# A two-layer decoder on one core: experts' outputs as rows in DRAM with gathers, three overlapping groups, a new preparation, and masks in half-array matmuls

## The chip, the cores and the metric

The kernel runs on one core of a Trainium2 chip. The metric is the time of one execution on the device in microseconds; three runs of the kernel before took 2507.99, 2510.61 and 2510.91 us (median 2510.61). Engines are named as in the profile: PE (TensorE matmul) with PEld (its weight loads), DVE (VectorE), ACT (ScalarE), POOL (GpSimd) and SP (SyncE, which here only issues DMAs).

## The reference

The input x is 64 batches of 128 tokens of 128 channels, in float32. Six blocks follow one another, each adding to x: self attention of 16 heads with a tanh cap, cross attention to 77 context tokens, and a gated feed-forward with weights quantized in groups of 16 (layer 0); a self attention with softplus weights, a cross-attention block, and a mixture of experts (layer 1). The parts that the change touches are these.

```
# layer 0, cross attention: a mask of integers, 0 or 1, per query and key
logits = q @ k.T / sqrt(dh) + (1 - mask) * -1e9      # 16 heads, 128 x 77 per batch
attn   = softmax(logits) * group_prob
# layer 0, feed-forward: each weight is quantized once, in groups of 16
sc8 = e4m3(max|w| / 6 * s);  q = sign(w) * nearest_fp4(|w| / dq) * dq
# layer 1, mixture of experts, per batch: 128 tokens, 8 experts, 2 per token, 38 slots per expert
p, e = top2(x @ router_w + router_b); p = softmax(p)
pos  = running count of e over (first choices, then second choices) - 1
inp[e, pos] += x                                     # a choice beyond slot 37 is dropped
o = (silu((inp @ w_fc + b_fc) * (inp @ w_gate + b_gate))) @ w_proj + b_proj   # 128 -> 512 -> 128
x = x + p0 * o[e0, pos0] + p1 * o[e1, pos1]          # an index beyond the last slot reads slot 37
```

## The kernel before

x stays in SBUF the whole time, as `x_resident` (tokens on partitions, 64 x 128 columns). The program is seven stages with a barrier of all engines between them: `prepare`, `l0_attention`, `l0_cross`, `l0_ffn`, `l1_attention`, `l1_cross` and `moe`. Inside a stage each engine has its own instruction stream, written out by hand, and the streams are held together by semaphores that only count up. Every engine works through its stream in order, so an instruction that waits holds all behind it.

`prepare` loads constants, weights and biases. SyncE issues the loads one by one (constants first, then the broadcast biases, the direct weights, the weights to be transposed, the three weights to be quantized, `wv` and `wp`), and after them the eight loads of x. All compute engines wait for one count over all of these loads (N_IN). PE transposes 18 weight blocks, VectorE finds the maximum of the three weights, whose reciprocal goes through PE to all partitions (L1022 to L1071), folds some weights (L1076 to L1092), and then `quantize` (L764) runs three times on VectorE, once per weight, 17 operations each that wait for one another. At the end VectorE waits for all of x.

`l0_cross` works on quads of 4 batches, with a software pipeline: `segment(c, h, p, l)` holds what each engine does for the quads at four stages. For each batch PE first writes the mask into four PSUM banks with `far` (two diagonal matrices of different size, as a single f16 can't hold the value) times `neg` (mask minus one, L1205), then adds the scores on 32-row parts of the array (L1209). VectorE takes maxima (L1476), subtracts (L1482) and sums (L1488), ScalarE takes exponentials, POOL multiplies with the gate (L1408) and the reciprocal (L1415), PE turns the weights (L1221) and multiplies with the values (L1234). VectorE makes `neg` once per quad (L1461).

`moe` works on groups of 8 batches (304 slots per expert), one pass of its loop per group. In 32 steps k (8 experts times 4 parts of the hidden 512) PE multiplies the slots of expert k//4 with w_fc and w_gate (`hidden`, L2811 and L2814), ScalarE adds the bias (L2912), VectorE adds the other bias and multiplies (L3056), ScalarE applies silu (L2919), and three steps later PE projects (`project`, L2823) with the output's channels on partitions; ScalarE moves each expert's output to `oT` (L2923). Between the steps the routing of the next group is placed: statistics and normalising on VectorE, transposes (L2777), router (L2783), top 2 (`choose`), counts (`places`) and positions (`finish`). Also between the steps VectorE builds for each batch a combine matrix of tokens by slots that holds the two probabilities (`combine`, L3042 to L3046), which PE turns (L2831) and ScalarE copies (L2928). After the steps comes a part without experts' work: for each batch PE turns the outputs to rows (L2861), ScalarE copies them (L2949), PE multiplies combine matrix and rows (L2875), VectorE adds to x (L3073), and PE makes the slots of the next group (`dispatch`, L2802) from the matrices that VectorE builds (L3032, L3034), copied by ScalarE (L2904). The next group's first step waits for all of this, as `xt`, the slots' buffer, exists once.

## Time and profile before

| | |
|---|---|
| median of three runs | 2510.61 us |
| the profiled execution | 2510.06 us |
| its span, first to last instruction | 2508.3 us |
| busy share of PE, PEld, DVE, ACT, POOL | 75%, 54%, 70%, 58%, 46% |
| mean granted clock of TensorE | 0.861 of full speed |
| DMA | 29.90 MB, mean 12 GB/s |

The stages follow one another without overlap: `prepare` to 61 us, `l0_attention` to 446, `l0_cross` to 882, `l0_ffn` to 1191, `l1_attention` to 1442, `l1_cross` to 1846, `moe` to the end. Busy shares over the whole span say little, since each stage has its own limit; a stage is read from a stretch in its middle, and from what its busiest engine waits for. A line of a timeline gives start, length, engine, line in the kernel, operation and tiles; a number behind x is how many records were merged, and brackets hold the idle time before it and what ended it. A float32 matmul has two records, one per pass. Lengths of matmuls include the way through the array, so the distance of two starts is what the engine takes for one.

### The profile page before, as it was taken

The numbers are of one execution on the slowest core, as the hardware profiler recorded it, in microseconds if no ns is written. First come the engines' busy times: TensorE is split into PE (matmuls) and PEld (weight loads), VectorE is DVE, ScalarE is ACT, GpSimd is POOL, SyncE is SP. The second block draws the span as 40 slices with busy tenths as digits, with TensorE's granted clock in tenths as the row PEclk, the third lists the DMA queues.
The fourth block names the chain that finished last, engine by engine and source line by source line (L and its number), as shares of the span: only waits on it lengthen the run. The fifth ranks groups of instructions, "written<-read, shape, count | busy, mean of one in ns | idle before, by whom it ended". The sixth has DMA issues, their size and how long they took to land. (4 is left out here: it accounts for less than half of the span.)

```text
span 2508.3 us, 50896 instructions
## 1 busy us (share of the span) xinstructions
PE 1885.9 (75%) x16165; PEld 1365.9 (54%) x16174; DVE 1762.3 (70%) x4140; ACT 1458.9 (58%) x2564; POOL 1141.6 (46%) x1090
## 2 busy tenths in 40 slices
PE   1677777699999924444556569999858988889888
PEld 1455555476767602222334347777636666666666
DVE  4799996588888679997555548888845555455553
ACT  1588887477777644554222257777725565565654
POOL 1466665488888748876111047888820000000000
PEclk7699998699999955555777779999979999999999
DMA  4000000100000030000000000000000000000000
GB/s 131 1 1 0 0 0 2 27 18 21 17 21 18 4 101 0 0 0 1 0 0 0 0 16 8 5 8 5 1 1 1 9 8 8 0 8 8 8 8 9
DMA packets 54153, 29.90 MB, mean 12 GB/s; under 512 B 18776, under 2 KB 50608, under 8 KB 54064
## 3 DMA queue, kind: packets, MB, share of 16 engines
q1 hardware_dynamic: 53920, 28.75, 4.2%
q8 instruction: 46, 0.75, 0.1%
q14 instruction: 43, 0.35, 0.0%
q10 hardware_dynamic: 144, 0.05, 0.0%
HBM read 24.60 MB, written 4.19 MB: 11 GB/s over the span
## 5 line engine op out<-in xcount | busy, mean ns | idle before, releaser
L3056 DVE SCALAR_TENSOR_TENSOR m_z<-psum,bias_col,m_hb 128x304 f32<-128x304 f32 x256 | 134.4, 532 | 208.1 <-ACT m_hb L2912 199.8
L2912 ACT ACTIVATE m_hb<-psum,bias_col 128x304 f32<-128x304 f32 x256 | 131.0, 512 | 171.6 <-PE psum L2811 171.0
L182 POOL TENSOR_SCALAR mln_ve<-mln_mv 128x4 f32<-128x4 f32 x16 | 4.5, 281 | 490.1 <-DVE mln_mv L149 490.1
L2811 PE MATMUL psum<-m_xt,w_fc 128*128 128x304 f32 x512 | 175.5, 424 | 4.5 <-ACT m_xt L2904 4.5
L1408 POOL TENSOR_TENSOR x_gated<-x_score,x_gate 128x1232 f32<-128x1232 f32 x64 | 166.5, 2601 | 22.0 <-ACT x_score L1343 18.6
L2814 PE MATMUL psum<-m_xt,w_gate 128*128 128x304 f32 x512 | 175.0, 423 | 0.0
L2823 PE MATMUL psum<-m_hid,w_proj 128*128 128x304 f32 x512 | 172.2, 423 | 0.0
L1350 ACT COPY x_pT<-psum 77x512 f32<-77x512 f32 x256 | 136.2, 583 | 57.7 <-PE psum L1221 57.4
L1415 POOL TENSOR_TENSOR x_gated<-x_gated,x_rden 128x1232 f32<-128x1232 f32 x64 | 143.9, 2248 | 44.0 <-DVE x_rden L1494 38.8
L463 POOL TENSOR_SCALAR_AFFINE_SELECT a_prob<-a_prob 128x1024 f32<-128x1024 f32 x128 | 137.7, 1098 | 54.4 <-ACT a_prob L508 53.7
L502 ACT ACTIVATE a_prob<-psum 128x1024 f32<-128x1024 f32 x128 | 129.6, 1029 | 49.7 <-PE psum L612 29.7
L1221 PE MATMUL psum<-const,x_gated 128*77 128x128 f32 x1024 | 137.0, 277 | 4.3 <-ACT x_pT L1350 2.4
L1221 PEld LDWEIGHTS psum<-const,x_gated 128*77 128x77 f32 x1024 | 115.7, 148 | 36.1 <-issue 21.6
L508 ACT ACTIVATE a_prob<-a_prob 128x1024 f32<-128x1024 f32 x128 | 134.5, 1068 | 0.1
L2919 ACT ACTIVATE m_hid<-m_z 128x304 f32<-128x304 f32 x256 | 115.0, 449 | 15.9 <-DVE m_z L3056 14.8
L1476 DVE TENSOR_REDUCE x_mx<-psum 128x16 f32<-128x1232 f32 x64 | 91.8, 1434 | 43.0 <-PE psum L1209 43.0
L2814 PEld LDWEIGHTS psum<-m_xt,w_gate 128*128 128x128 f32 x512 | 96.4, 190 | 37.1 <-DVE m_z L3056 5.0
L2823 PEld LDWEIGHTS psum<-m_hid,w_proj 128*128 128x128 f32 x512 | 96.7, 191 | 34.3 <-ACT m_hid L2919 2.1
L1616 PE MATMUL psum<-wq,f_xqT 128*128 128x512 bf16 x64 | 38.0, 594 | 93.5 <-DVE f_h L1844 67.3
L2811 PEld LDWEIGHTS psum<-m_xt,w_fc 128*128 128x128 f32 x512 | 90.4, 191 | 30.1 <-ACT m_xt L2904 8.3
L1488 DVE TENSOR_REDUCE x_den<-x_score 128x16 f32<-128x1232 f32 x64 | 91.3, 1427 | 16.2 <-ACT x_score L1343 16.2
L2046 POOL TENSOR_SCALAR_AFFINE_SELECT a_wt<-a_wt 128x512 f32<-128x512 f32 x16 | 9.9, 636 | 195.0 <-DVE a_wt L2072 195.0
(400 smaller groups left out, 5675.5 us busy)
## 6 DMA issues: line engine op xcount, KB each, us to landing
x_ctx<-in_ctx_dram SPq DMA_DIRECT2D x32, 154.0 KB
x_resident<-in_x_dram SPq DMA_DIRECT2D x8, 512.0 KB, 7.3
out_dram<-x_resident SPq DMA_DIRECT2D x8, 512.0 KB, 3.2
x_mask<-in_mask_BxSxS_ik_dram SPq DMA_DIRECT2D x16, 154.0 KB, 2.9
x_gate<-in_fside_BxSxS_dram SPq DMA_DIRECT2D x16, 154.0 KB, 2.6
w_fc<-in_L_ffn_w_c_fc_dram SPq DMA_DIRECT2D x1, 2048.0 KB, 10.3
w_gate<-in_L_ffn_w_gate_dram SPq DMA_DIRECT2D x1, 2048.0 KB, 15.4
const<-in_const_dram SPq DMA_DIRECT2D x1, 607.0 KB, 3.6
```

The lines of the kernel that those rows point to most:

```text
L463: pool.affine_select(out=v, in_=v, compare_op=ALU.is_ge, fill=0.0, base=0, pattern=[[0, 8], [1, P]], channel_multiplier=-1).then_inc(sem[" ...
L502: act.activation(prob[:, m % RING, :], psum[:, b0:b0 + 2, :].rearrange("p g t -> p (g t)"), ACT.Tanh, scale=S_SCALE).then_inc(sem["tanh"], UH)
L508: act.activation(v, v, ACT.Exp, scale=CAP).then_inc(sem["p"], UH)
L1221: ins = pe.transpose(psum[0:NCTX, TURN + j % 2, g * P:(g + 1) * P], gated[:, n % 2, at:at + NCTX], core.ident)
L1350: act.copy(pT[0:NCTX, n % 2, j, :], psum[0:NCTX, TURN + j % 2, :]).then_inc(sem["pT"], 1)
L1408: pool.tensor_tensor(heads(gated[:, n % 2, :]), heads(score[:, n, :]), bc(gate[q.s][:, n, :], 1, H), ALU.mult).then_inc(sem["gated"], UB)
L1415: pool.tensor_tensor(g, g, bc(rden[:, n % 2, :], 2, NCTX), ALU.mult).then_inc(sem["weighted"], UB)
L2811: pe.matmul(psum[:, 2 + k % 2, 0:N * K], core.w_fc[:, e, f * P:(f + 1) * P], rhs, start=True, stop=True).then_inc(sem["h_ps"], PER_STEP)
L2814: pe.matmul(psum[:, 4 + k % 2, 0:N * K], core.w_gate[:, e, f * P:(f + 1) * P], rhs, start=True, stop=True).then_inc(sem["g_ps"], PER_STEP)
L2823: ins = pe.matmul(psum[:, 6 + e % 2, 0:N * K], core.w_proj[:, e, f, :], hid[:, k % 4, :], start=(f == 0), stop=(f == NF - 1))
L2912: act.activation(hb[:, k % 2, :], psum[:, 2 + k % 2, 0:N * K], ACT.Identity, bias=bias[:, fcb + k:fcb + k + 1]).then_inc(sem["h"], PER_STEP)
L3056: dve.scalar_tensor_tensor(out=z[:, k % 2, :], in0=psum[:, 4 + k % 2, 0:N * K], scalar=bias[:, gb + k:gb + k + 1], in1=hb[:, k % 2, :], op ...
```

## The change

1. `prepare`. SyncE issues the three weights to be quantized and the constants first (count q_in), then the other weights (w_in), then x, whose first load has its own semaphore `x_first`. The broadcast biases are issued from ScalarE's queue behind the rows of biases (small_in). VectorE starts with the maxima of all groups of 16 of all three weights, the trip through PE goes ahead of the transposes, the small operations of quantizing run once over the three weights together, and the rounding to the grid uses ScalarE's Abs and two operations of VectorE. The foldings come after. The statistics of the third quad in `l0_attention`, not the end of `prepare`, wait for the rest of x.
2. `l0_cross`. One matrix `far` of 128 x 64 holds both diagonals, one on each half of the partitions; the mask is loaded so that each half of the partitions holds each half of the queries (four DMAs a quad instead of one, twice the bytes), and `neg` is twice as long. Each of the eight matmuls has 64 output rows.
3. `moe`. The projection has the roles of its operands exchanged: three pieces of 102 slots as weights, 128 channels as moving columns, so that PSUM holds rows of slots. VectorE adds the bias from a broadcast tile and evicts (`out_rows`), SyncE writes the rows to DRAM (`write_rows`), and POOL gathers for each batch and each of the two choices the 128 rows of its tokens with an indirect DMA (`gather`, 16 per group). VectorE combines with two multiply-adds per batch into x (`combine`). The combine matrices, their transposes, the turned rows and the matmuls of the tail are gone. A period of 32 steps holds the experts of group g, the routing and dispatch of g+1 and the combining of g-1, with two buffers of slots and of DRAM rows; the loop's body is two periods. The second probability comes from Tanh of half the difference instead of Exp. The dispatch, router and count matmuls share one PSUM bank, the output has three.

The core of the diff:

```diff
+            for dst, src in q_loads:
+                sp.dma_start(dst, src).then_inc(sem["q_in"], 16)
+            for dst, src in w_loads:
+                sp.dma_start(dst, src).then_inc(sem["w_in"], 16)
             x_dram = inp["x"].rearrange("b t c -> t b c")
             for q in range(core.n_batch // PER_ITER):
                 n = PER_ITER
                 sp.dma_start(core.x[:, q * n * C:(q + 1) * n * C].rearrange("p (b c) -> p b c", b=n),
-                             x_dram[:, q * n:(q + 1) * n, :]).then_inc(core.x_in, 16)
+                             x_dram[:, q * n:(q + 1) * n, :]).then_inc(core.x_first if q == 0 else core.x_in, 16)
...
+            for dst, src in loads:
+                act.dma_start(dst, src).then_inc(sem["small_in"], 16)
+            for k in range(3):
+                act.wait_ge(sem["scaled"], k + 1)
+                if GRID_BANK[k] == 3:
+                    act.wait_ge(sem["max_bc"], 1)
+                act.activation(psum[:, GRID_BANK[k], :], qa[:, 4 * k * P:4 * (k + 1) * P], ACT.Abs, scale=GRID).then_inc(sem["grid"], 1)
...
+            link(dve.tensor_reduce(amax[:], groups(qraw[:]), AX_X, ALU.max, apply_absolute_value=True))
+            dve.tensor_reduce(mx[:], by_weight(amax[:]), AX_X, ALU.max).then_inc(sem["max"], 1)
+            dve.tensor_copy(core.ident16[:], core.ident).then_inc(sem["ident16"], 1)
+            dve.wait_ge(sem["max_ps"], 1)
...
+            link(dve.tensor_scalar(scale[:], scale[:], FP8_MAX, None, ALU.min))
+            link(dve.tensor_scalar(u32(power[:]), u32(scale[:]), 0x7F800000, None, ALU.bitwise_and))
+            link(dve.tensor_scalar(power[:], power[:], 2.0 ** -6, 1.5 * 2.0 ** 20, ALU.max, ALU.mult))
+            link(dve.tensor_tensor(scale[:], scale[:], power[:], ALU.add))
+            link(dve.tensor_tensor(sc8[:], power[:], scale[:], ALU.subtract))
+            link(dve.tensor_scalar(power[:], sc8[:], -1.0, 2.0 ** -9, ALU.mult, ALU.max))
+            link(dve.reciprocal(inv[:], power[:]))
+            link(dve.tensor_tensor(by_weight(inv[:]), by_weight(inv[:]), bc(gs[:], 2, NG), ALU.mult))
+            link(dve.tensor_scalar(inv[:], inv[:], 1.0 + 2.0 ** -23, None, ALU.mult))
+            part = lambda ap, k: ap[:, 4 * k * P:4 * (k + 1) * P]
+            for k in range(3):
+                dve.tensor_tensor(groups(part(qa[:], k)), groups(part(qraw[:], k)), bc(inv[:, k * NG:(k + 1) * NG], 2, 16),
+                                  ALU.mult).then_inc(sem["scaled"], 1)
+            for k in range(3):
+                a, q, grid = part(qa[:], k), part(wq[:], k), psum[:, GRID_BANK[k], :]
+                dve.wait_ge(sem["grid"], k + 1)
+                dve.wait_ge(sem["scaled"], k + 1)
+                link(dve.scalar_tensor_tensor(out=a, in0=grid, scalar=GRID, in1=a, op0=ALU.max, op1=ALU.add))
+                link(dve.scalar_tensor_tensor(out=q, in0=grid, scalar=GRID, in1=a, op0=ALU.max, op1=ALU.subtract))
+                link(dve.tensor_scalar(q, q, FP4_MAX, -FP4_MAX, ALU.min, ALU.max))
+                dve.tensor_tensor(groups(q), groups(q), bc(sc8[:, k * NG:(k + 1) * NG], 2, 16), ALU.mult).then_inc(sem["wq_ready"], 1)
...
+                for k in range(2):
+                    for half in range(2):
+                        sp.dma_start(mask[s][64 * k:64 * k + 64, half], rows("mask_BxSxS2_ik1", t)[64 * half:64 * half + 64]
+                                     ).then_inc(sem[f"mask_in{s}"], 16)
...
-                for k in range(2):
-                    for g in range(4):
-                        pe.matmul(psum[:, S_BANK + g, 0:W].rearrange("p (j m) -> p j m", m=NCTX), core.far[k][:],
-                                  bc(neg[q.s][:, n, :], 1, J), start=(k == 0), stop=False)
+                for g in range(4):
+                    for k in range(2):
+                        r = slice(64 * k, 64 * k + 64)
+                        pe.matmul(psum[r, S_BANK + g, 0:W].rearrange("p (j m) -> p j m", m=NCTX), core.far[:],
+                                  bc(neg[q.s][:, k, n, :], 1, J), start=True, stop=False)
...
+        def groups(engine, period):
+            period(1, 0, True, False)
+            with engine.Fori(1, 2 + (N_GROUPS - 4) * STEP, 2 * STEP) as i:
+                period(i + STEP, 1, True, True)
+                period(i + 2 * STEP, 0, True, True)
+            period(1 + (N_GROUPS - 1) * STEP, 1, False, True)
+        AFTER = 1 + N_GROUPS * STEP
...
+            def write_rows(i, s, e):
+                sp.wait_ge(sem["orow"], i + BATCH * (e + 1))
+                sp.dma_start(rows[s][e * W:(e + 1) * W, :].rearrange("(j p) c -> p j c", p=PIECE), orow[:, e % 2, :, :]
+                             ).then_inc(sem[f"rows{e % 2}"], 16)
...
+            def project(i, k, behind):
+                e, f = k // NF, k % NF
+                pe.wait_ge(sem["act"], i + k + 1)
+                for j in range(PIECES):
+                    if f == 0 and (behind or e > 0):
+                        pe.wait_ge(sem["orow"], i + BATCH * (e - 1) + (BATCH if j == LAST else j + 1))
+                    ins = pe.matmul(psum[0:PIECE, O_BANK + j, 0:C], hid[:, k % 4, j * PIECE:(j + 1) * PIECE], core.w_proj[:, e, f, :],
                                     start=(f == 0), stop=(f == NF - 1))
+                ins.then_inc(sem["o_ps"], 1)
...
+                        if k in (7, 8):
+                            turn_input(i + STEP, k - 7)
+                        if k == 10:
+                            router(i + STEP)
+                        if k == 14:
+                            places(i + STEP)
+                        if 18 <= k < 18 + N:
+                            dispatch(i + STEP, k - 18)
...
+            def gather(i, s):
+                for buffer in range(2):
+                    pool.wait_ge(sem[f"rows{buffer}"], 2 * (i - 1) + 2 * STEP)
+                pool.wait_ge(sem["number"], i + STEP)
+                pool.wait_ge(sem["x_out"], i)
+                pool.wait_ge(sem["ready"], i)
+                pool.tensor_tensor(spare[:], core.one[:], core.one[:], ALU.mult).then_inc(sem["ready"], STEP)
+                for n in range(N):
+                    for k in range(2):
+                        pool.indirect_dma_start(got[:, k, n, :], None, rows[s], bass.IndirectOffsetOnAxis(ap=number[:, k, n:n + 1], axis=0)
+                                                ).then_inc(sem[f"got{n // QUAD}"], 16)
...
+            def out_rows(i, e, behind):
+                dve.wait_ge(sem["o_ps"], i + NF * (e + 1))
+                dve.wait_ge(sem["bias_in"], 16)
+                if behind or e >= 2:
+                    dve.wait_ge(sem[f"rows{e % 2}"], 2 * (i - 1) + 16 * (e // 2))
+                for j in range(PIECES):
+                    dve.tensor_tensor(orow[:, e % 2, j, :], psum[0:PIECE, O_BANK + j, 0:C], b_proj[0:PIECE, e, :], ALU.add
+                                      ).then_inc(sem["orow"], BATCH - LAST if j == LAST else 1)
+            def take(i, s):
+                dve.wait_ge(sem["x_out"], i)
+                dve.wait_ge(sem["prob"], i + STEP)
+                dve.tensor_copy(weight[:], prob[:, s, :, :]).then_inc(sem["taken"], STEP)
+                dve.tensor_copy(number[:], back[:, s, :, :]).then_inc(sem["number"], STEP)
+            def combine(i, n):
+                if n % QUAD == 0:
+                    dve.wait_ge(sem[f"got{n // QUAD}"], 4 * (i - 1) + 4 * STEP)
+                    dve.wait_ge(sem["taken"], i + STEP)
+                x = core.x_cols(i, n // QUAD, n % QUAD)
+                dve.scalar_tensor_tensor(out=x, in0=got[:, 0, n, :], scalar=weight[:, 0, n:n + 1], in1=x, op0=ALU.mult,
+                                         op1=ALU.add).then_inc(sem["half"], BATCH)
+                dve.wait_ge(sem["half"], i + BATCH * (n + 1))
+                dve.scalar_tensor_tensor(out=x, in0=got[:, 1, n, :], scalar=weight[:, 1, n:n + 1], in1=x, op0=ALU.mult,
+                                         op1=ALU.add).then_inc(sem["x_out"], BATCH)
...
+                    if k >= LAG - 1 and (k - LAG + 1) % NF == 0 and k >= LAG + NF - 1:
+                        out_rows(i, (k - LAG + 1) // NF - 1, behind)
+                    if behind:
+                        if k == 0:
+                            take(i - STEP, 1 - s)
+                        if k == LAG - 1:
+                            out_rows(i - STEP, E - 1, True)
+                        if k >= STEPS - N:
+                            combine(i - STEP, k - STEPS + N)
                     if ahead:
+                        if k in (1, 3):
+                            statistics(i + STEP, k // 2)
+                        if k in (5, 6):
+                            normalise(i + STEP, k - 5)
+                        if k == 11:
+                            largest(i + STEP)
+                        if k == 12:
+                            choose(i + STEP)
+                        if k == 15:
+                            probabilities(i + STEP, 1 - s)
+                        if k == 16:
+                            positions(i + STEP, 1 - s)
+                        if 17 <= k < 17 + N:
+                            slots(i + STEP, k - 17)
```

## Rows read from the trace of the kernel before

**Rows 1.** One group's stretch: length, busy PE, PEld, DVE, ACT, POOL, clock.

```profile
2115.70:2194.66 78.96, 69.54 (x331) 51.12 (x331) 43.04 (x141) 46.70 (x104) 2.83 (x4) 1.00 0.02 7
```

**Rows 2.** One line's instructions: ns min/median/max, first and last start.

```profile
L2811 PE MATMUL psum<-m_xt,w_fc x512: 419/419/711, 1876.0 to 2487.9; 128*128 128x304 f32 x171
```

**Rows 3.** Timeline of PE in the steps: start, length in us.

```profile
2122.49 0.68 PE L2811 MATMUL psum<-m_xt,w_fc 128*128 128x304 f32 x2
...
2124.02 0.68 PE L2811 MATMUL psum<-m_xt,w_fc 128*128 128x304 f32 x2
```

**Rows 4.** Timeline of PE where a group ends and another begins.

```profile
2191.58 0.83 PE L2875 MATMUL psum<-m_orow,m_ct 114*128 114x128 f32 x6
...
2192.25 0.68 PE L2802 MATMUL psum<-m_disp,m_xn 128*128 128x304 f32 x2
...
2194.66 0.78 PE L2811 MATMUL psum<-m_xt,w_fc 128*128 128x304 f32 x2 [0.56 <-ACT m_xt L2904]
```

**Rows 5.** Groups by line in rows 1's window: busy, mean | idle before.

```profile
L2831 PE MATMUL psum<-const,m_comb 128*114 128x128 f32 x24 | 4.1, 279 | 7.7 <-ACT m_ct L2928 7.7
...
L2783 PE MATMUL psum<-w_router,m_xnT 128*128 128x8 f32 x16 | 1.8, 251 | 0.0
...
L2904 ACT COPY m_xt<-psum 128x304 f32<-128x304 f32 x8 | 3.3, 413 | 6.9 <-PE psum L2802 6.9
...
L184 POOL TENSOR_TENSOR mln_rstd<-mln_ve,minus_half 128x4 f32<-128x4 f32 x2 | 2.3, 1138 | 0.3
```

**Rows 6.** Timeline of one step, PE and ScalarE.

```profile
2169.84 0.68 PE L2811 MATMUL psum<-m_xt,w_fc 128*128 128x304 f32 x2
...
2170.56 0.52 ACT L2912 ACTIVATE m_hb<-psum,bias_col 128x304 f32<-128x304 f32 x1 [1.21 <-PE psum L2811]
...
2170.97 0.45 ACT L2919 ACTIVATE m_hid<-m_z 128x304 f32<-128x304 f32 x1
```

**Rows 7.** Last work of the run, from VectorE's timeline.

```profile
2502.73 0.69 DVE L3073 TENSOR_TENSOR x_resident<-x_resident,psum 128x512 f32<-128x512 f32 x1 [4.04 <-PE psum L2875]
```

**Rows 8.** DMA issues: count, KB, median us from issue to landing.

```profile
out_dram<-x_resident SPq DMA_DIRECT2D x8, 512.0 KB, 3.2
...
su_raw<-in_L_attn_Wv_dram SPq DMA_DIRECT2D x1, 64.0 KB, 2.2
```

**Rows 9.** Timeline of SyncE's queue in the preparation.

```profile
21.31 0.43 SPq L944 DMA_DIRECT2D su_wp<-in_L_attn_Wp_dram  x1
```

**Rows 10.** Timeline of VectorE in the preparation and just after it.

```profile
25.00 1.75 DVE L1056 TENSOR_REDUCE su_mx<-su_qraw 128x3 f32<-128x1536 f32 x1 [23.93 <-DMA su_wp<-in_L_attn_Wp_dram]
...
35.17 0.67 DVE L777 TENSOR_REDUCE su_t_amax<-su_qraw 128x32 f32<-128x512 f32 x1
...
56.53 0.69 DVE L800 TENSOR_TENSOR su_wq<-su_t_a,su_t_sc 128x512 bf16<-128x512 f32 x1
60.95 0.87 DVE L258 BATCH_NORM_STATS2 a0ln_stats<-x_resident 128x6 f32<-128x128 f32 x4 [3.73 <-PEq L71]
```

**Rows 11.** `x_resident` on VectorE: one addition per quad of layer 0's cross attention.

```profile
L1499 DVE TENSOR_TENSOR x_resident<-x_resident,psum x16: 673/674/686, 514.9 to 879.5; 128x512 f32 x12, 128x512 f32<-128x512 f32 x4
```

**Rows 12.** A stretch of that stage, columns as rows 1.

```profile
600.00:624.30 24.30, 22.77 (x278) 17.16 (x276) 20.61 (x27) 17.14 (x31) 20.69 (x12) 1.00 0.08 19
```

**Rows 13.** Timeline of that stage, all engines.

```profile
638.13 2.25 POOL L1415 TENSOR_TENSOR x_gated<-x_gated,x_rden 128x1232 f32<-128x1232 f32 x1
639.33 1.23 DVE L1461 TENSOR_SCALAR x_neg<-x_mask 128x308 f16<-128x308 int32 x1
...
646.14 1.08 PE L1234 MATMUL psum<-x_pT,x_v 77*32 77x128 f32 x32
...
648.36 1.26 PE L1205 MATMUL psum<-x_neg,far 128*128 128x308 f16 x8
...
649.55 0.80 PE L1209 MATMUL psum<-x_kexp,x_qT 32*128 32x308 f32 x8
```

**Rows 14.** `x_neg` on VectorE: ns min/median/max, first and last start.

```profile
L1461 DVE TENSOR_SCALAR x_neg<-x_mask x16: 307/1254/2459, 450.5 to 815.2; 128x308 f16<-128x308 int32 x16
```

562 lines of the change are left out of this document (250 added, 312 removed), and 1 row of the table BIAS_ROWS.

## The prediction

> **What bounds the kernel now.** I read the stretches by stage first, then for each changed stage the timeline and the groups by line, then the list of DMA issues. The span is 2508.3 us and the profiled execution took 2510.06 us, 1.8 more; the three timed runs have their median 0.5 us above that.
>
> The last stage is the longest piece. Its first expert matmul starts at 1876.0 [rows 2], so experts, combining and the final store fill the last 632.3 us. One group of 8 batches takes 78.96 us, in which PE is busy 69.54, VectorE 43 and ScalarE 47, at a full clock [rows 1]: PE sets the pace. The reader is to see in it three sorts of time. The 32 steps are three matmuls of 304 columns each, one step every 1.53 us (0.51 per matmul) [rows 3], 49 us. The combining costs PE the transposes of the combine matrix with 7.7 us of idle time before them, because each waits for a ScalarE copy [rows 5], and a tail after the last step in which rows are turned and multiplied. The rest is routing, the dispatch matmuls and small waits.
>
> In the preparation VectorE does nothing before 25.00, when the last of the loads (issued at 21.31) lands, and then runs one serial chain to 57.22, after which the next stage starts at 60.95 [rows 9, 10]. In layer 0's cross attention a quad takes (879.5 - 514.9)/15 = 24.3 us [rows 11], of which PE is busy 22.77, VectorE 20.61, POOL 20.69 [rows 12]: PE first, two others close behind.
>
> **The preparation: -28 us.** (a) The three quantized weights and the constants now are the first four loads. The loads came 0.475 apart (45 issues by 21.31) and the last landed 3.7 us after its issue [rows 9, 10], so the fourth is issued at about 2.2 and lands at 6; as these four are large (1.4 MB, where a 512 KB store takes 3.2 us [rows 8]) I take 8. VectorE starts 17.0 earlier. (b) From 25.00 to 35.17 ran the maximum, its trip over PE, and foldings that wait for transposed weights [rows 10]. The trip stays and the foldings still cost their 4 us, but no transposes stand in between: 8 instead of 10.2, -2.2. (c) Three quantizing chains took 57.22 - 35.17 = 22.05, each 7.3 [rows 10]. Now the ten small operations run once over three weights (3.2 us: ten of 0.25 to 0.7), then come three scalings of 0.69 and three times four operations of up to 0.69 with their waits (7.9): 13.2, -8.8. ScalarE's Abs and PE's transposes lie beside it. (d) POOL's rows of bvo follow VectorE by some 3 us, while the last transposes no longer trail: the gap of 3.7 us to the next stage stays within 1. Sum 28.0. The first x load now only has to land for the first group, at about 20; the rest is wanted only by the third quad. Bounds: -20, if the broadcast loads that now leave ScalarE's queue hold the weights back, to -31.
>
> **Cross attention: -15 us.** Eight mask matmuls of 308 columns stand 649.55 - 648.36 = 1.19 us ahead of the score matmuls [rows 13]; 8 x 0.128 at full rate is 1.03. Now each has 64 output columns, and the two of one bank go to different halves of the array. That column groups run beside each other is seen in the value matmuls: 32 passes of 128 columns in 1.08 us [rows 13], where one after the other would be 1.7 even at one cycle per column (53 ns each). So 4 x 0.128 = 0.51 instead of 1.03, and 0.16 of switching twice instead of once: -0.35 to -0.5 per batch, -1.4 to -2.1 per quad on PE. Against it: the quad has only 24.3 - 22.8 = 1.5 us of slack on PE, but VectorE needs more than 20.6 [rows 12], and its mask conversion doubles. That conversion is 307 ns at least and 1254 ns in the median [rows 14]: at 639.33 it lasts until POOL's multiplication of 638.13 ends, at 640.38 [rows 13]. Waiting there stays, and 308 more elements add about 0.2. VectorE's and POOL's chains thus keep part of the gain: I take -0.95 per quad, 16 quads, -15. Ends: -33 (all of PE's) and 0.
>
> Here the Trainium skill speaks against the change. "TensorEngine Tiling (Array Packing)", Key Properties, says that changing the tiling mode drains the engine; the rows show 0.16 us over the sum for one such switch, and by the rule the gain would be nearer 0.35 than 0.5 per batch. Its page "SBUF — State Buffer" says that VectorE's two-port operations and GpSimd block each other entirely; the conversion that ends with POOL's operation agrees.
>
> **The last stage: -84 us.** (a) Gone are the transposes of combine matrices and their waits, the turned rows, and the matmuls of the tail. (b) A step now is two matmuls of 306 columns, 1.03 us, and a projection of three pieces, each 128 columns with 102 weight columns. Six passes of that shape take 2192.25 - 2191.58 = 0.67 us [rows 4]. Step: 1.70, 32 steps 54.4. (c) Between the steps: eight dispatches at 0.51 (304 columns as in rows 3), 4.1; the router 1.8 [rows 5]; eleven small matmuls for input and places at no more than 1.8/16 each, 1.2. (d) Waits: the dispatches share one bank. ScalarE's first operation starts 0.72 after PE's, the second at 1.13 [rows 6], the copy follows at about 1.5 and takes 0.41 [rows 5], so the next dispatch starts at 1.95 where PE is ready at 1.70: 8 x 0.25 = 2.0. The second input transpose waits 0.5; table loads and the rest 1.0. T = 54.4 + 7.1 + 3.5 = 65.0. ScalarE has 37 and VectorE (32 x 0.57, slots 7.6, row bias 5.6, combining 4.8, routing 9) some 46: neither is the bound. The output bank is single: the eviction of three pieces (0.8 us) lies beside the next two hidden matmuls (1.03); without that cover it would cost 0.8 x 8 a group.
>
> (e) The gathers on POOL. No indirect DMA is in the trace. From below each costs POOL the 0.43 us of an issue [rows 9]; from above, issue and landing of a 64 KB load one after the other, 0.43 + 2.2 [rows 8, 9], or beside a write's landing 3.2, even 4.3. I take d = 1.1, POOL's own pow on 4 elements (1.138 us [rows 5]), as POOL generates these in software. A group's 16 gathers start when the last expert's rows have landed, about 9 us into the period, and take 17.6; they are wanted at step 24, at 47 us. They are hidden while 9 + 16d + 2 stays below the second half's 54: d < 2.7.
>
> (f) Order of the whole: first group 4 us later (a dispatch waits for each copy), seven periods of 65.0, a last without routing 55.5, three last projections 2.0. Then nothing covers the drain: eviction 0.9, rows landed 3.2, a POOL operation 0.6, 16d = 17.6, landing 2.2, four batches combined 2.4, and from the last addition's end (2503.42 [rows 7]) to the end of the span 4.9: 31.8. Sum 548.3 against 632.3: -84.
>
> Forecast: 2508.3 - 28 - 15 - 84 = 2381.3, with 1.8 around it 2383.
>
> **Rivals.**
> A: the gathers pace the stage. The loop is 16d, landing 2.2, four steps of combining 6.8, three steps to the last rows 5.9, write 3.2: T = 16d + 18. If a gather holds POOL until it has landed, d = 1.1 + 2.2 = 3.3 and T = 70.8: 7 x 5.8 and 16 x 2.2 in the drain, +76: 2459. For it: nothing in the trace shows POOL issuing ahead. Against: SyncE's issues are 0.475 apart and land 3.7 later, so queues run ahead of landings. The "SBUF — State Buffer" page says that descriptors of POOL's DMAs starve while VectorE runs a two-port operation, which lengthens d; rows 14 show the lock with an ordinary POOL operation only.
> B, slower than before: the same loop with d from 3.7 (7(16d - 47) + 16(d - 1.1) = 127). At 4.3, a gather that waits for a memory round trip as the 3.2 us store [rows 8], T = 86.8, 7 x 21.8 + 51 = +204: 2587. It decides at d = 3.7.
> C: the cross attention gains nothing (VectorE and POOL bound it) and PE loses 1 us more a group in waits: +15 + 8, 2406. For it: both engines at 20.6 of 24.3.
> D: PE's waits in the groups are smaller and the mask gain full: -18 - 14: 2351.
>
> **How the numbers follow.** Forecast 0.60, C 0.17, D 0.08, A 0.09, B 0.05, the change undone by something else within 5 us of before 0.01. The range goes from D's side to beyond C, with d up to 2.2 in the drain (+18): 2348 to 2432. What measurement of this kernel can tell from no change is 0.2%, 5 us. Faster: all but B and the last, 0.93; same 0.02; slower 0.05.
>
> **What would show it.** The first statistics of layer 0's attention near 33 us, with q loads landed near 8. Mask matmuls to score matmuls 0.7 to 0.85 us apart, a quad near 23.3. PE steps of 1.70, T near 65, no PE wait for VectorE's combining. POOL's gathers 1.1 us apart, the drain 32 us. It would be wrong if gathers are over 2.7 us apart, if the 102-column pieces take more than 0.67, or if a table load falls into each period's steps.

## The result and the profile after

The changed kernel takes 2497.3 us (median of 10 runs; the kernel before beside it 2511.2), a ratio of 0.9935 with a 95% interval of 0.9919 to 0.9951. One of the ten took 2905 us at a granted clock of 0.61, and the ratio leaves it out. The change makes the kernel 0.65% faster; the forecast was 2383 us. Its profiled execution took 2497.56 us with a span of 2495.8.

The stages ahead of the last one gave 33 us by this trace, where 43 were forecast. The last stage, forecast to become 84 us shorter, became 15.6 us longer, counted from its first expert matmul (20.8 counted from the end of the stage ahead of it): its first expert matmul starts at 1847.9 (28.1 us earlier than [rows 2]) and the span ends at 2495.8, 647.9 later. First the stretches between the casts on VectorE that begin each group's combining (`m_number`, at 1915.05, 1993.23, 2073.46, 2150.41, 2234.39, 2311.58, 2390.14, 2460.72), columns as in [rows 1]: a period without gathers, two with, the last without routing, and the drain.

```profile
1847.90:1915.05 67.15, 65.59 (x357) 52.23 (x358) 37.19 (x138) 32.80 (x77) 2.53 (x4) 0.96 0.07 17
1993.23:2073.46 80.23, 68.85 (x376) 55.26 (x374) 42.26 (x159) 31.47 (x76) 17.97 (x21) 0.94 0.17 43
2073.46:2150.41 76.95, 65.21 (x352) 51.46 (x353) 42.06 (x159) 30.55 (x74) 18.19 (x21) 0.91 0.12 30
2390.14:2460.72 70.58, 57.46 (x329) 47.11 (x327) 27.65 (x78) 27.19 (x63) 15.32 (x17) 0.90 0.17 44
2460.72:2495.80 35.08, 0.00 (x0) 0.00 (x0) 5.27 (x19) 0.00 (x0) 15.34 (x17) 0.55 0.22 58
```

The first period, which has nothing to gather, takes 67.2 us; the six with gathers take 475.1, 79.2 each, the last 70.6 where 55.5 were forecast. Compare the two stretches with gathers with the same two of g_paced below (67.88 and 63.29 us), a kernel without the loss: VectorE and ScalarE are busy as long, PE 3.5 and 3.8 us longer, out of 12.4 and 13.7 us. Most of the missing time is idle time. In the third stretch POOL's gathers run from 2080.86 to 2100.78, 1.25 us apart in the main (here the first, third, fourth and last of 16):

```profile
2080.86 1.11 POOL L2958 DMA_INDIRECT m_got<-m_rows,m_number  x1 [0.36 <-issue]
...
2083.52 1.04 POOL L2958 DMA_INDIRECT m_got<-m_rows,m_number  x1 [0.30 <-issue]
2084.86 0.94 POOL L2958 DMA_INDIRECT m_got<-m_rows,m_number  x1 [0.30 <-issue]
...
2099.84 0.94 POOL L2958 DMA_INDIRECT m_got<-m_rows,m_number  x1 [0.30 <-issue]
```

and these are PE, ScalarE and VectorE in that time:

```profile
2088.97 0.68 PE L2846 MATMUL psum<-m_xt,w_fc 128*128 128x306 f32 x2
2089.49 0.68 PE L2850 MATMUL psum<-m_xt,w_gate 128*128 128x306 f32 x2
2090.00 0.82 PE L2859 MATMUL psum<-w_proj,m_hid 128*102 128x128 f32 x6
...
2094.07 0.76 PE L2846 MATMUL psum<-m_xt,w_fc 128*128 128x306 f32 x2
...
2104.09 1.58 PE L2859 MATMUL psum<-w_proj,m_hid 128*102 128x128 f32 x6 [7.39 <-DVE m_orow L3060]
```

```profile
2085.10 0.52 ACT L2914 ACTIVATE m_hb<-psum,bias_col 128x306 f32<-128x306 f32 x1 [1.78 <-PE psum L2846]
...
2090.88 0.52 ACT L2914 ACTIVATE m_hb<-psum,bias_col 128x306 f32<-128x306 f32 x1 [4.44 <-PE psum L2846]
...
2100.06 0.52 ACT L2914 ACTIVATE m_hb<-psum,bias_col 128x306 f32<-128x306 f32 x1 [7.84 <-remote]
```

```profile
2091.43 0.54 DVE L3051 SCALAR_TENSOR_TENSOR m_z<-psum,bias_col,m_hb 128x306 f32<-128x306 f32 x1 [5.24 <-issue]
2102.95 0.54 DVE L3051 SCALAR_TENSOR_TENSOR m_z<-psum,bias_col,m_hb 128x306 f32<-128x306 f32 x1 [10.99 <-remote]
```

The three engines stand still together, and not for each other in a way that the code explains. PE's matmul of 2094.07 should release ScalarE 0.7 us later, as [rows 6] show of before; ScalarE starts at 2100.06. An engine tells another that an operation is done by raising a semaphore, here called an update, and the trace records the updates. ScalarE's and VectorE's, where recorded, come 0.01 us after their operation's end in every step of the stage. TensorE's come 0.01 us after it outside the gathers, and during a burst from the third or fourth gather on up to 10 us late: that of the matmul of 2094.07 is recorded at 2100.04, ScalarE's start. Only in those stretches records of updates are missing at all: 75 of the 1548 of a step's six semaphores, 19 of TensorE's and 56 of ScalarE's and VectorE's. Where ScalarE's record is missing VectorE follows at once all the same (2091.43, ScalarE's 0.52 us from 2090.88 just over), so a missing record is not a late update. A matmul's end is modelled in a profile, so an update that comes late and a matmul that truly ends late would look alike; the matmuls behind it start at their usual distance (2088.97, 2089.49, 2090.00 above), which speaks for the update. When the burst ends, all run again within 2 to 5 us. The granted clock of these two periods is 0.94 and 0.91, where [rows 1] had 1.00: behind the idle 7.39 us the six projection matmuls take 1.58 us for 0.82, at a granted clock of 0.50 (2104.0 to 2105.7), the 1.2 GHz level, so some of the loss comes on top of the waiting.

In the preparation VectorE's chain runs as forecast and then waits:

```profile
8.61 1.75 DVE L1035 TENSOR_REDUCE su_amax<-su_qraw 128x96 f32<-128x1536 f32 x1 [7.54 <-DMA const<-in_const_dram]
...
24.88 0.71 DVE L1066 TENSOR_TENSOR su_wq<-su_wq,su_sc 128x512 bf16<-128x512 bf16 x1
...
32.51 0.29 DVE L1080 TENSOR_TENSOR b_x_bvo<-psum,b_sa_b 128x128 f32<-128x128 f32 x1 [5.34 <-PE psum L1014]
...
38.90 0.87 DVE L258 BATCH_NORM_STATS2 a0ln_stats<-x_resident 128x6 f32<-128x128 f32 x4 [4.29 <-PEq L71]
```

```profile
23.20 4.03 PE L996 MATMUL psum<-const,su_raw 128*128 128x128 f32 x18 [10.82 <-DMA w_router<-in_L_ffn_router_w_dram]
```

The quantizing is over at 25.6, but PE's 18 transposes start only at 23.20, when the last of the other weights has landed, and the foldings behind them hold VectorE until 32.51. In the cross attention the mask matmuls now stand 0.67 us ahead of the score matmuls (1.19 in [rows 13]), a quad takes 23.75 us by the additions to x, of which the first starts at 486.2 and the last at 842.4 (24.3 by [rows 11]), and in one quad PE is busy 21.56, VectorE 20.78 and POOL 20.93 (22.77, 20.61, 20.69 in [rows 12]):

```profile
L1503 DVE TENSOR_TENSOR x_resident<-x_resident,psum x16: 673/675/687, 486.2 to 842.4; 128x512 f32 x12, 128x512 f32<-128x512 f32 x4
```

```profile
603.11 0.74 PE L1209 MATMUL psum<-x_neg,far 128*64 128x308 f16 x8
603.78 0.80 PE L1213 MATMUL psum<-x_kexp,x_qT 32*128 32x308 f32 x8
```

### The profile page after: what moved, and what is told of

Same layout as the page of the kernel before. It is cut to its first block and busy times, and to the rows that moved or that the text cites. A ratio compares the mean times of both kernels' runs of the same rounds, so it can differ in the third digit from the quotient of the medians.

```text
span 2495.8 us, 51220 instructions
## 1 busy us (share of the span) xinstructions
PE 1844.8 (74%) x16430; PEld 1363.0 (55%) x16430; DVE 1751.4 (70%) x4251; ACT 1340.3 (54%) x2348; POOL 1264.6 (51%) x1234
## 3 DMA queue, kind: packets, MB, share of 16 engines
q10 hardware_dynamic: 2432, 0.90, 0.2%
## 5 line engine op out<-in xcount | busy, mean ns | idle before, releaser
L2914 ACT ACTIVATE m_hb<-psum,bias_col 128x306 f32<-128x306 f32 x256 | 132.1, 516 | 361.0 <-PE psum L2846 256.2
L3051 DVE SCALAR_TENSOR_TENSOR m_z<-psum,bias_col,m_hb 128x306 f32<-128x306 f32 x256 | 136.9, 535 | 267.5 <-ACT m_hb L2914 139.2
L2859 PEld LDWEIGHTS psum<-w_proj,m_hid 128*102 128x102 f32 x1536 | 203.5, 173 | 75.2 <-issue 33.0
L2859 PE MATMUL psum<-w_proj,m_hid 128*102 128x128 f32 x1536 | 215.8, 278 | 30.5 <-DVE m_orow L3060 30.5
L2846 PE MATMUL psum<-m_xt,w_fc 128*128 128x306 f32 x512 | 184.1, 442 | 2.6 <-issue 1.9
L2850 PE MATMUL psum<-m_xt,w_gate 128*128 128x306 f32 x512 | 181.7, 437 | 4.2 <-issue 2.3
L2958 POOL DMA_INDIRECT m_got<-m_rows,m_number x128 | 122.1, 954 | 41.3 <-issue 41.3
L2921 ACT ACTIVATE m_hid<-m_z 128x306 f32<-128x306 f32 x256 | 114.9, 449 | 4.0 <-DVE m_z L3051 4.0
L1480 DVE TENSOR_REDUCE x_mx<-psum 128x16 f32<-128x1232 f32 x64 | 91.8, 1435 | 23.4 <-PE psum L1213 22.8
L1620 PE MATMUL psum<-wq,f_xqT 128*128 128x512 bf16 x64 | 37.8, 590 | 87.1 <-DVE f_h L1848 64.9
```

Of the source, the lines that this page charges most:

```text
L2846: pe.matmul(psum[:, H_BANK + k % 2, 0:W], core.w_fc[:, e, f * P:(f + 1) * P], xt[s][:, e, :], start=True, stop=True).then_inc(sem["h_ps"], 1)
L2850: pe.matmul(psum[:, G_BANK + k % 2, 0:W], core.w_gate[:, e, f * P:(f + 1) * P], xt[s][:, e, :], start=True, stop=True).then_inc(sem["g_ps" ...
L2859: ins = pe.matmul(psum[0:PIECE, O_BANK + j, 0:C], hid[:, k % 4, j * PIECE:(j + 1) * PIECE], core.w_proj[:, e, f, :], start=(f == 0), stop= ...
L2921: act.activation(hid[:, k % 4, :], z[:, k % 2, :], ACT.Silu).then_inc(sem["act"], 1)
L2958: pool.indirect_dma_start(got[:, k, n, :], None, rows[s], bass.IndirectOffsetOnAxis(ap=number[:, k, n:n + 1], axis=0)).then_inc(sem[f"got{ ...
L3051: dve.scalar_tensor_tensor(out=z[:, k % 2, :], in0=psum[:, G_BANK + k % 2, 0:W], scalar=bias[:, gb + k:gb + k + 1], in1=hb[:, k % 2, :], o ...
```

## Experiments

All are the changed kernel with one edit, or another experiment's kernel with one edit more where that is said; medians of 4 to 10 runs beside the kernel before (2508.2 to 2509.3). Those that leave out a part of the result (g_none, g_plain, g_sync, g_few, s2_half, g_busy) are there for their time alone. First: are the gathers the cause, and what of them? **g_none** drops them:

```diff
-                for n in range(N):
-                    for k in range(2):
-                        pool.indirect_dma_start(got[:, k, n, :], None, rows[s], ...)
```

> The changed kernel without its 128 gathers (everything POOL waits for ahead of them stays; the combination reads a buffer of zeros, so that part of the result is left out). Theory 'descriptors' (POOL's preparing of indirect gathers holds up the other engines) and theory 'traffic' (1 MB of 512-byte rows per period delays them) both give: periods of 66 us (the first one of the changed kernel, which has no gathers, takes 67.2) in place of 77 to 84, a last period of 55 in place of 70.6, a drain 20 us shorter: 2380 to 2395 us. Theory 'place' (the stall of 12 to 15 us belongs to the code at steps 4 to 15 of a period, to the routing between them or to TensorE's clock, and not to the gathers): periods stay at 77 to 80, only the drain shortens: 2475 to 2485 us.

2373.3 us: the periods are 65.4, 67.6, 63.7, 67.6, 63.7, 64.6 and the last 55.0. The stall is the gathers'; "place" falls. **g_plain** and **g_sync** move the same bytes without looking rows up, from POOL and from SyncE:

```diff
-    pool.indirect_dma_start(got[:, k, n, :], None, rows[s], ...)
+    pool.dma_start(got[:, k, n, :], rows[s][n * P + 64 * k:n * P + 64 * k + P, :])     # g_plain
+    sp.dma_start(got[:, k, n, :], rows[s][n * P + 64 * k:n * P + 64 * k + P, :])       # g_sync, in SyncE's order
```

> The changed kernel with the 16 indirect gathers of a period replaced, at the same place in POOL's order and behind the same waits, by 16 plain copies of 128 rows of 512 bytes from the same buffer (fixed rows in place of the looked-up ones: the choice of rows is left out). 'Descriptors', if only looked-up rows are costly to prepare: periods 66 to 68, 2385 to 2410 us. 'Descriptors', if whatever POOL issues is prepared in software: periods as before, 77 to 80, 2480 to 2500. 'Traffic': 77 to 80, 2480 to 2500, and g_sync the same. 'Place': 2475 to 2500.

> As g_plain, but the 16 copies of a period are issued by SyncE, behind its last write of rows, with the same waits. The same 1 MB moves in the same stretch, and POOL does nothing in it. 'Descriptors': the stall is gone, periods 66 to 68, 2385 to 2410 us. 'Traffic': periods stay at 77 to 80, 2480 to 2500. 'Place': the same as 'traffic' here, told apart by g_none.

2384.3 and 2379.3 us, the seven periods 447.6 and 447.1 us together, as the 447.6 without any: the copies cost nothing but their place in the drain. 1 MB moved by POOL's own queue in 8.4 us (a copy every 0.53) disturbs nobody, so "traffic" falls. **g_paced** keeps the gathers and spreads them:

```diff
+    PACED = [4 + (3 * j) // 2 for j in range(2 * N)]
...
+    pool.wait_ge(sem["z"], i + STEP + PACED[2 * n + k])
+    pool.tensor_tensor(spare[:, j:j + 1], core.one[:], core.one[:], ALU.mult).then_inc(sem["ready"], 1)
     pool.indirect_dma_start(got[:, k, n, :], None, rows[s], ...)
```

(j is 2n + k; the last group's gathers stay as they were.)

> The changed kernel with its gathers spread over the period: POOL waits for the expert step 4 + 3j/2 of the current group ahead of gather j (16 small operations more per period), so that one gather goes out every 1.5 steps (2.5 us) in place of every 1.25 us; the last group's go out at once as before. If each gather holds the others up for about 1 us on its own (75% of 1.25 us by the stall of 15 us over 16 gathers), and the cost adds up whatever its spacing: periods 77 to 80 as before, 2490 to 2505 us. If a step has slack between two operations of the binding engine that a short hold-up falls into, or if only gathers close behind one another stall: periods 67 to 72, 2400 to 2450 us. 'Traffic' also allows the second, since the rate halves.

2394.3 us, ratio 0.9554 (0.9530 to 0.9579). The stall is gone, and this is the first complete version that is well ahead of both kernels. Two of its periods, as the second and third stretch above; PE's clock is 1.00 in both:

```profile
1974.25:2042.13 67.88, 65.37 (x376) 52.48 (x374) 42.71 (x159) 31.47 (x76) 21.86 (x37) 1.00 0.19 51
2042.13:2105.42 63.29, 61.40 (x352) 49.46 (x353) 42.25 (x159) 30.53 (x74) 22.11 (x37) 1.00 0.14 37
```

The six periods take 392.3 us, 65.4 each, the last 55.0. **g_step** and **g_fours** set `PACED` to `4 + j` and to `4 + 6 * (j // 4)`:

> As g_paced, with one gather per expert step (gather j behind step 4 + j, 1.69 us apart in place of 2.5; back to back they are 1.25 us apart). Theory 'no room' (the updates that engines send each other get through only while no gather is being prepared; 0.3 us in 1.25 is too little room, 0.7 us in 1.69 enough): periods of 65 us as in g_paced, whose mean was 64.97 us, 2390 to 2400 us. If instead what is held up grows with the rate (share of POOL's time in gathers: 75% back to back, 38% in g_paced, 56% here): some 4 to 8 us per period, 2420 to 2450 us.

> The paced kernel with its gathers in four bunches: four back to back every six steps (10 us), so the mean rate of g_paced with the spacing of the changed kernel inside a bunch. If what counts is the gap between two gathers: each bunch of 5 us holds the others up for 2.5 to 4 us, 10 to 15 us a period as in the changed kernel, 2460 to 2500 us. If a hold-up has to build up over many gathers: periods of 65 to 68 us, 2390 to 2415 us.

2394.6 and 2397.4 us, no late update of TensorE in either trace. Neither one gather every 1.69 us nor bunches of four hurt. More than that, in g_step the first eight gathers of a period ran only 1.35 us apart and were free too. **g_few** leaves the burst as it is and gathers 16 rows with each instruction (`got[0:16, k, n, :]`, `number[0:16, k, n:n + 1]`):

> The changed kernel with its 16 gathers of a period back to back as they are, but of 16 rows each in place of 128 (the other 112 partitions keep zeros: that part of the result is left out). If a gather's 954 ns are its rows' (7.5 ns a row), a gather falls to about 120 to 250 ns, the stretch to 6 us, and the stall with it: 2373 to 2390 us. If they are the instruction's, the stretch stays at 20 us; then the stall stays if it comes from POOL preparing (2480 to 2500), and goes if it comes from the 128 requests (2380 to 2400).

2396.6 us, periods of 63.3 to 68.2 like g_paced's, although its gathers take 0.85 us each and 1.15 from one to the next: the 954 ns are the instruction's, hardly the rows', and the stall goes with the rows. **g_busy** puts arithmetic in place of the gathers in g_none (`pool.tensor_tensor` on 128x512, 16 times, each waiting for the one before it):

> The kernel of g_none (no gathers, 2373.3 us) with 16 multiplications of 128x512 on POOL in their place, each behind the one before it, 16 to 20 us in all: POOL is as busy as with gathers, with arithmetic. Theory 'port' (DVE and POOL keep each other from the buffer): DVE's operations at that place get longer by tenths of a us and the period grows by 3 to 15 us, 2395 to 2480 us. Theory 'gathers alone': 2370 to 2380 us, as without them.

2429.0 us, 55.7 more than g_none, periods of 69 to 74. A stall, but another one: no update of TensorE is late, and VectorE's normalising (`m_xn`) takes the time, here g_busy and then g_none (ns min/median/max):

```profile
L190 DVE TENSOR_SCALAR m_xn<-x_resident,mln_mv,mln_rstd x64: 329/1292/1308, 1815.9 to 2289.0; 128x128 f32 x48, 128x128 f32<-128x128 f32 x16
```

```profile
L190 DVE TENSOR_SCALAR m_xn<-x_resident,mln_mv,mln_rstd x64: 335/340/352, 1816.2 to 2252.4; 128x128 f32 x48, 128x128 f32<-128x128 f32 x16
```

Eight of them a period, 340 ns alone and up to one POOL multiplication (1278) beside it: of the 5.2 us by which the third period grew, 4.8 are these. That is the lock of [rows 14]. It agrees with the Trainium skill's "SBUF — State Buffer", Who interferes with whom, by which two-port VectorE operations and GpSimd block each other. With gathers in its place the same operation keeps 345 ns in the mean of the stalled third period, so the gathers' stall is not this lock.

What is it in the burst? **g_spacer** puts g_paced's small operation between the gathers and leaves the wait out; **g_late** holds the unbroken burst back (`pool.wait_ge(sem["z"], i + STEP + 11)` once, ahead of all 16):

> The changed kernel with one small POOL operation (a product of 128x1, 193 ns) ahead of each gather and no pacing: the 16 gathers of a period go out in one burst. In g_step the first eight gathers of a period ran 1.35 us apart, with that operation between, against 1.25 us in the changed kernel, and nothing stalled. Theory 'unbroken run' (only gathers that follow one another directly on POOL hold TensorE up): no stall, periods of 65 us, 2392 to 2400 us. Theory 'many in one run' (it needs more than eight gathers at this density, whatever stands between them): stall of 5 to 12 us a period, 2430 to 2490 us.

> The changed kernel with its unbroken burst of 16 gathers held back until step 11 of the current group's experts is done (one wait more), so that it lies over steps 11 to 23 (token choice, prefix sums, first dispatches) in place of steps 3 to 14 (transposes, router). If the stall belongs to the burst: 10 to 15 us a period as in the changed kernel, now beside those steps, 2470 to 2510 us. If it belongs to the work of steps 3 to 14 (TensorE's transposes and router products) meeting the burst: periods of 65 to 68 us, 2390 to 2415 us.

g_spacer 2466.7: periods of 74 to 78, some 70% of what g_paced gains is lost again; "unbroken run" falls. g_late 2512.8: periods of 80 to 85, the stall goes where the burst goes. **s2_ready** and **s2_const** put a wait between that has long been met:

```diff
+    pool.wait_ge(sem["number"], i + STEP)     # s2_ready, ahead of g_spacer's small operation
+    pool.wait_ge(sem["blank"], 1)             # s2_const, on the gather itself
```

> The kernel of g_spacer (2466.7 us; small operation ahead of every gather, one burst) with a wait ahead of that operation that has long been met, against a register's value as in g_step (on the semaphore of the row numbers in place of the expert step). Theory 'a wait between' (POOL's sequencer has to stop at each gather, and that alone lets the others through): no stall, periods of 65 us, 2390 to 2400 us. Theory 'length of the burst' (g_step and g_paced are free of it because their bursts pause after four to eight gathers): as g_spacer, periods of 74 to 78 us, 2460 to 2475 us.

> The changed kernel with a wait that has long been met, against a constant, on each gather itself, and nothing else between them. 'A wait between' in its general form: no stall or a smaller one, 2390 to 2470 us. If only a wait that the sequencer works out from a register helps, or none: as the changed kernel, 2490 to 2505 us.

2466.6 (g_spacer again) and 2493.8 (the changed kernel again): a met wait does nothing. **s2_half** gathers 64 rows with each instruction, **s2_fours** is g_fours with the wait and the operation only ahead of every fourth gather:

> The changed kernel with its 16 gathers of a period back to back, of 64 rows each in place of 128 (the other 64 partitions keep zeros: that part of the result is left out). In g_few, gathers of 16 rows took 0.85 us each, 1.15 apart, and nothing stalled. If the stall grows with the rows that a burst asks for: about half of the 12 us a period, 2420 to 2450 us. If there is a limit that 128 rows at this rate pass and 64 do not: 2388 to 2400 us. If the number of gathers decides and g_few was free for another reason (rows of partitions 0 to 15 alone): 2480 to 2500.

> The kernel of g_fours (2397.4 us) without the wait and the small operation inside a bunch: four gathers of 128 rows directly behind one another, every six steps. 'Length of the burst': in the changed kernel TensorE's first late update comes 2.5 to 4.6 us after the burst's start, and a bunch ends at 4.7 us, so a bunch is nearly free, periods of 65 to 68 us, 2392 to 2415 us. 'A wait between': each bunch stalls for the share of the changed kernel (12 of 20 us), 2 to 3 us a bunch, 8 to 12 a period, 2440 to 2475 us.

s2_half 2506.0, as bad as 128 rows (2497.3) or worse: not in proportion to rows. Somewhere between 16 and 64 rows it begins. s2_fours 2401.7, periods of 63.5 to 69.3: some 1 us a period is lost, and 22 of 258 records of one TensorE semaphore are missing, as only in the stalled kernels. In the third period's first bunch an update of TensorE, due at 2059.45, is recorded 1.1 us late. So four unbroken gathers already touch it.

Then the traces gave the idea: what POOL's sequencer does, the part that hands the instructions to the engine and works ahead of it (`POOLq` in the rows). The row that shows it is the register operation (`ALU_OP`) behind the 16th gather, in the changed kernel over 2075 to 2110, where the burst starts at 2080.86:

```profile
L181 POOLq ALU_OP  x2: 32/32/32, 2075.8 to 2087.4; - x2
```

At 2087.4 the sequencer is through with all 16, and the engine is in its sixth. (In g_few it runs as far ahead, 6.6 us into the burst, and nothing stalls: it takes the larger gathers too.) In g_spacer the same row comes at 2088.9, 13.4 us into a burst that starts at 2075.51, with the engine in its tenth gather. **s_chain** takes that running ahead away: s2_ready's wait, on the small operation just before.

```diff
-    pool.wait_ge(sem["number"], i + STEP)
+    pool.wait_ge(sem["ready"], i + STEP - 2 * N + 2 * n + k)
```

> The kernel of s2_ready (2466.6 us) with one value changed: ahead of each gather POOL waits for the small operation of the gather before it (of the same engine), in place of a wait long met. The 16 gathers stay one burst, 1.36 to 1.5 us apart, but the sequencer is at most one gather ahead of the engine. Theory 'running ahead': no late update of TensorE, periods of 65 us, 2390 to 2402 us. Theory 'length of the burst': as s2_ready and g_spacer, periods of 73 to 78 us, 2455 to 2475 us.

2395.6 us, ratio 0.9557 (0.9537 to 0.9577), periods of 65.0, 67.7, 63.3, 67.7, 63.3, 64.9 and no late or missing update (of the updates of POOL's small operation too all 122 are recorded, where s2_ready has 44 of 122). The gathers lie as densely as in s2_ready (2466.6 us), and the sequencer works out its waits in step with them, eight between 2051.4 and 2059.9 (burst from 2051.65):

```profile
2054.57 0.98 POOL L2961 DMA_INDIRECT m_got<-m_rows,m_number  x1 [0.15 <-issue]
2055.56 0.21 POOL L2960 TENSOR_TENSOR m_spare<-one 128x1 f32<-128x1 f32 x1
2055.92 0.98 POOL L2961 DMA_INDIRECT m_got<-m_rows,m_number  x1 [0.15 <-issue]
```

```profile
L2959 POOLq ALU_OP  x8: 32/32/32, 2051.4 to 2059.9; - x8
```

The two kernels differ in one wait. Length, density, bytes and rows are equal; what differs is how far the sequencer may be ahead, and with it one small thing that no run takes apart: s_chain works out the wait's value ahead of every gather (32 ns of the sequencer each), s2_ready has no such operation between its gathers. **s_eights** lets it run through eight (`PACED` is `4 + 12 * (j // 8)`, the wait only at j = 0 and 8):

> As g_fours (2397.4 us), with two bunches of eight gathers, at steps 4 and 16, a small operation ahead of each gather and the wait for the step ahead of a bunch alone, so the sequencer runs ahead through all eight. 'Running ahead': late updates from the third or fourth gather of a bunch on, half to all of g_spacer's 10 us a period, periods of 69 to 75 us, 2420 to 2465 us. 'Length of the burst' with a limit over eight (g_step's first eight were free): periods of 65 us, 2392 to 2402 us.

2399.0 us, periods like g_paced's, no late update: my expectation for "running ahead" missed. The sequencer did run ahead; it works out the second bunch's wait 3.2 us into the first bunch (from 2050.13), with the engine in its third gather:

```profile
L2962 POOLq ALU_OP  x2: 32/32/32, 2049.3 to 2053.3; - x2
```

So five gathers wait there and nothing stalls, while g_spacer, where some six wait when the sequencer is through, loses 10 us a period. With an operation between, a run of eight is free and a run of sixteen is not; without one, a run of four already costs something. How far ahead, counted in gathers, is thus not the whole rule: holding the sequencer back is shown to be enough, and so is breaking the run up. The limit is left open, as is the mechanism that ties TensorE's updates to gathers waiting on POOL. One rival is untested: every execution timed here has its span and clock from the profiler, and the stall comes where records get lost, so that the recording takes part in it is not excluded.

Last, the other two parts. **c_mask** is g_paced with the mask products of before (and their load and conversion of the mask), **m_old** the changed kernel with the last stage of before:

```diff
-    pe.matmul(psum[r, S_BANK + g, 0:W]..., core.far[:], bc(neg[q.s][:, k, n, :], 1, J), start=True, stop=False)
+    pe.matmul(psum[:, S_BANK + g, 0:W]..., core.far[k][:], bc(neg[q.s][:, n, :], 1, J), start=(k == 0), stop=False)
```

> The kernel of g_paced (2394.3 us) with the mask products of the layer-0 cross attention as before: one load of the mask, full-height products into all 128 rows, two per bank summed. The trace of the changed kernel puts the stage 11.7 us shorter than before: theory 'all of it from the mask products': 2403 to 2409 us. Rival, that the shorter stage comes from the different start of the resident input's loads or from code placement: 2392 to 2398 us.

> The changed kernel with the last stage of before (and its row of bias loads): the new preparation and the new mask products alone. By the stage boundaries of the two traces (the last stage starts 33.3 us earlier) it takes 2511 - 33 = 2474 to 2480 us: the changed last stage then costs 20 us against the old one in the changed kernel, and gains 80 us in g_paced. If the stages depend on each other (code placement, TensorE's clock left behind by one stage), it differs by more than 4 us.

c_mask 2410.7: the mask products are worth 16.4 us by the timed runs, of which 12.3 lie in the stage itself in the two traces (433.9 and 421.6 us from its first statistics to those of the next stage); the rest lies in stages of the same code. m_old 2468.8, 40.2 below before (0.9844, 0.9828 to 0.9860), 5 less than the low end expected from the stage boundaries. Neither expectation held to the microsecond: stage boundaries of the same code differ by 2 to 6 us from one profiled run to the next (the cross attention's last addition starts at 842.4 and 836.5 in the changed kernel and g_paced). The changed last stage costs 28.5 us as it was written and gains 74.5 in g_paced.

## Why the prediction was wrong

**The gathers, step (e).** They were priced by POOL's time alone: 1.1 us each, hidden below 2.7 apart. They came 1.25 apart and no combining waited for them within the loop, so by the step's own test they were hidden. What failed is what that test takes for granted, that work on an engine with slack costs the other engines nothing: the sum has no term for it, and no row gave a reason to put it at nothing. The runs show it at 103.0 us (2497.3 as written, 2394.3 with the same gathers paced, 2395.6 with POOL's sequencer held back). In the forecast's terms, six periods took 79.2 us in place of 65.0 (85) and the last 70.6 in place of 55.5 (15), 100 of the 114 us by which 2383 was missed. The rest: the first matmul came 28.1 us earlier, where 43 less the first group's 4 were forecast (11), and the first period and the drain took 3.5 more. None of the rivals had it: A and B price d, which was right. The range's upper end, 2432, was set by d too.

**The last stage's other steps** held. Without the stall (g_paced) a period is 65.4 where 65.0 was forecast, the last 55.0 (55.5), a plain step 1.69 (1.70). The output bank's eviction was covered. The first period takes 67.2, the drain from the cast on 35.1, where the forecast has 31.8 and three projections of 2.0 before it; gathers there are 1.38 apart. The first matmul comes 33.7 us after the stage before ends (28.5 before): +5.2 for the forecast +4.

**The preparation, -28**: the first statistics start 22.0 us earlier (38.90 for 60.95 in [rows 10]), layer 0's attention ends 25.4 earlier, and m_old and c_mask together leave it 40.2 - 16.4 = 23.8 (27.9 with the 12.3 of the traces). Only 22.0 of it come from the chain that (a) to (d) add up; layer 0's attention itself ran 3.4 us shorter in this trace and 5.6 in g_paced's, which no step had forecast, so the closeness to 28 is in part luck. The three quantizing chains did what (a) and (c) say: start at 8.61 (8 forecast), 17.0 us in all (8 and 13.2 less the 4 of foldings, 17.2). Step (b) failed: "no transposes stand in between" holds, but they stand last. They wait for every weight, the last issued at 15.38 and landed at 23.2 (not 3.7 but 7.8 us after, with the loads of ScalarE's queue beside it), then come 4 us of transposes, and the foldings that wait for them are done at 34.6, so the first statistics start at 38.90 for the 33 forecast. The step's lower bound, -20, had named this: ScalarE's loads holding the weights back. The step should have asked what becomes late once the chain is short.

**The cross attention, -15**: 16.4 by c_mask's times, 12 by the traces. PE's gain per batch was 0.52 us, just over the upper end given, 2.1 per quad; of this a quad kept 0.55 in the changed kernel's trace (24.3 to 23.75), 0.85 between those of c_mask and g_paced (24.33 to 23.49) and 1.0 by their times, against the 0.95 taken. So the forecast is right in size, and no run pins it closer. That VectorE keeps a part fits the rows: the mask matmuls wait 35.0 us for its subtraction in the whole stage, 23.4 before. Rival C falls. The rule of the Trainium skill's "TensorEngine Tiling (Array Packing)", Key Properties, that a change of tiling mode drains the engine, would have left 0.35; over the 0.51 of four matmuls the rows show 0.16, as much as before with one switch, so no loss for a second.

**The rule on descriptors** that the prediction cited beside rival A from the Trainium skill's "SBUF — State Buffer", that POOL's DMAs starve beside two-port VectorE operations: 121 of the 128 gathers took 940 to 980 ns, among them gathers with VectorE's normalising beside them; of the seven longer ones, up to 1232 ns, six are the first of a burst. The price d did not move. That page speaks of POOL's DMAs being held; in these runs it is TensorE's updates that are.

## What to carry to other kernels

Price what a new kind of instruction does to the engines beside it, not only what it takes of its own; where no row shows it, that belongs in the range. When all engines idle together and the releaser named has long been done, look at what is new in that window and run it once without, once spread out. Where a run of looked-up DMAs stalls other engines, as 16 of 128 rows did here, issue each behind a wait that is not yet met (an expert step, or the issuing engine's own previous operation): with the small operation that carries it, it cost 0.1 us a gather here and gave back 102 to 103.

## What the hardware showed

- An indirect gather of 128 rows of 512 bytes takes POOL 944 ns and the next starts 1.25 us after it; of 16 rows 847 ns and 1.15. A plain copy of the same bytes from POOL takes 534 ns, spaced 0.53.
- Sixteen such gathers with nothing to hold POOL's sequencer go with TensorE's semaphore updates up to 10 us late (h and g matmuls of the steps) and with lost records; with the sequencer held to one gather ahead of the engine (s_chain), none are late or lost.
- ScalarE's `Tanh` between the `Silu` steps needs no table load: the changed stage has one, at 1851.8, where the stage before had four a period (2115.7, 2118.1, 2164.2 and 2166.1 in that of [rows 1]).
- POOL's sequencer got ten gathers ahead of the engine. The Trainium skill's "Advanced Engine Details and Errata", Engine Queue Depths, gives GpSimd a queue of 8; the row at 2087.4 shows ten gathers handed on and not begun, somewhat more.
- Copies of 1 MB into the same buffers in 8.4 us, issued by POOL, cost TensorE nothing, nor did those issued by SyncE. The Trainium skill's "SBUF — State Buffer", Who interferes with whom, says that DMA never contends with a compute engine: g_plain and g_sync agree. The bursts of gathers do hold TensorE up; whether that is contention of DMA is open.
